# One bonus instruction for numerator and denominator, and a recomputed last maximum, in a linear attention of five engines

## The reference

```python
def step(carry, kv_t):
    p, q, o = carry
    kt, vt = kv_t
    no = jnp.maximum(o, u + kt)
    A = jnp.exp(o - no)
    Bc = jnp.exp(u + kt - no)
    y = (A * p + Bc * vt) / (A * q + Bc)
    no2 = jnp.maximum(w + o, kt)
    A2 = jnp.exp(w + o - no2)
    B2 = jnp.exp(kt - no2)
    return ((A2 * p + B2 * vt, A2 * q + B2, no2), y)
```

## Time and profile before

| | us |
|---|---|
| median of 3 runs | 6002.13 |
| lowest, highest | 5991.86, 6011.43 |
| profiled execution, its own time | 6008.11 |
| its span, first to last instruction | 6006.3 |
| attention stage in it | 1698 to 3718 |
| VectorE busy over the span | 4211.5 (70%) |
| TensorE busy over the span | 4937.5 (82%) |

### The profile page before, as it was taken

The page is one execution under the profiler, slowest core; times in us unless marked ns, Lnnn a source line. Parts: engine busy times, 40 slices in busy tenths (PEclk is TensorE's granted clock), DMA queues, the critical chain, the costliest instruction groups (busy, mean ns, idle before and its releaser), DMA issues. The chain is left out here.

```text
span 6006.3 us, 77285 instructions
## 1 busy us (share of the span) xinstructions
PE 4937.5 (82%) x23504; PEld 3954.3 (66%) x23504; DVE 4211.5 (70%) x5193; ACT 3702.6 (62%) x6950; POOL 3425.7 (57%) x2796
## 2 busy tenths in 40 slices
PE   5969999958866766767667673788899999999999
PEld 5969999847632443433334332676788888888888
DVE  4427777789849898888888885897555555555555
ACT  0016666545557888888888884565565665656565
POOL 0019999835549687777777872454444444444444
PEclk9979999979988988888889886999999999999999
DMA  6977777578840223213212122887422322322320
GB/s 170 264 187 197 193 196 205 148 185 255 245 104 11 68 52 76 65 43 88 54 44 65 44 65 56 233 268 226 105 69 54 82 60 56 86 56 54 88 54 24
DMA packets 389868, 689.60 MB, mean 115 GB/s; under 512 B 22399, under 2 KB 347986, under 8 KB 370194
## 3 DMA queue, kind: packets, MB, share of 16 engines
q1 hardware_dynamic: 335184, 529.89, 36.6%
q10 hardware_dynamic: 54386, 156.21, 7.3%
HBM read 452.17 MB, written 233.87 MB: 114 GB/s over the span
## 5 line engine op out<-in xcount | busy, mean ns | idle before, releaser
L1543 POOL TENSOR_TENSOR hidden_part<-hidden_whole,hidden_part 128x448 fp32r<-128x448 f32 x672 | 751.5, 1154 | 1025.9 <-ACT hidden_part L1508 1025.7
L661 POOL TENSOR_TENSOR omni_in_part<-omni_norm,omni_in_part 118x448 fp32r<-118x448 f32 x384 | 466.0, 1215 | 555.5 <-ACT omni_in_part L723 539.7
L1412 PE MATMUL f_out_ps<-hidden_part,ffn_wv_parts 128*128 128x448 f32 (+1 forms) x3360 | 720.8, 370 | 0.7 <-POOL hidden_part L1543 0.7
L418 POOL TENSOR_TENSOR dw_band_part<-dw_band,dw_band_part 112x862 fp32r<-112x862 f32 x192 | 438.7, 2285 | 470.6 <-ACT dw_band_part L529 470.5
L1412 PEld LDWEIGHTS f_out_ps<-hidden_part,ffn_wv_parts 128*128 128x128 f32 (+1 forms) x3360 | 578.1, 177 | 103.7 <-POOL hidden_part L1543 35.1
L87 PE MATMUL omni_ps<-omni_in_part,omni_band_part 118*118 118x432 f32 (+1 forms) x1152 | 435.7, 378 | 236.2 <-DVE omni_band_part L693 218.4
L1217 POOL TENSOR_TENSOR input_times_v<-input_factor,v_all 128x448 f32<-128x448 f32 x336 | 419.6, 1249 | 362.8 <-ACT input_factor L1110 343.3
L1586 DVE TENSOR_SCALAR hidden_whole<-f_hid_ps 128x448 f32<-128x448 f32 x672 | 417.6, 622 | 250.5 <-POOL hidden_part L1543 155.9
L1039 PE MATMUL proj_ps<-mixT_low,kvr_weights_low 128*128 128x448 f32 x672 | 354.0, 611 | 203.9 <-ACT k_all L1101 174.1
L87 PE MATMUL dw_ps<-dw_in_part,dw_band_part 112*118 112x432 f32 (+3 forms) x1344 | 473.7, 352 | 57.4 <-POOL dw_in_part L488 57.4
L1041 PE MATMUL proj_ps<-mixT_ends,kvr_weights_ends 128*128 128x448 f32 x1008 | 515.3, 595 | 0.0
(11 more groups left out here) (183 smaller groups left out, 13650.6 us busy)
## 6 DMA issues: line engine op xcount, KB each, us to landing
dw_band<-flat SPq DMA_DIRECT2D x48, 1508.5 KB
xin<-x SPq DMA_DIRECT2D x16, 2352.0 KB, 13.1
x_pointwise<-xp ACTq DMA_DIRECT2D x16, 2352.0 KB, 18.9
dw_in<-x_pointwise SPq DMA_DIRECT2D x24, 1568.0 KB
y_gelu<-dw_out ACTq DMA_DIRECT2D x48, 784.0 KB
omni_in<-y_gelu SPq DMA_DIRECT2D x48, 784.0 KB
att_mix<-omni_out ACTq DMA_DIRECT2D x48, 784.0 KB
residual_pairs<-y_gelu SPq DMA_DIRECT2D x16, 2352.0 KB, 11.9
```

The costliest lines, as they stand in the source:

```text
L418: eng.tensor_tensor(rounded(p[1]), wt[u][0:parts, cc, :], p[0], ALU.subtract).then_inc(band_split, 1)
L661: pool.tensor_tensor(rounded(p[1][:, :, :]), z[u][:, cc], p[0][:, :, :], ALU.subtract).then_inc(in_split, 1)
L1412: return pe.matmul(bank, rounded(w), rounded(x), start=start, stop=stop)
L1543: pool.tensor_tensor(rounded(kk[n % 2][1][:, h, :]), whole[h % KW][:, :], kk[n % 2][0][:, h, :], ALU.subtract).then_inc(kl_ready, 1)
```

## The change

1. **One bonus instruction.** `input_factor` and `input_times_v` become the two halves of one buffer `input_factors` of 128 x 2 x 448, four of them. A single `scalar_tensor_tensor` over both halves and both PSUM banks does what L1282 and L1285 did. It waits for both scans, and one semaphore, `added`, takes the place of `d_done` and `n_done`; the log waits for it, and the division needs only the inverse. `weigh` now waits for the division of four units before instead of two (column units still also for the last division of the tile's rows).
2. **Row units recompute the last maximum.** From the second row unit of a pass on, the scan covers 449 cells: it starts one pixel earlier, from the former unit's maximum before its last pixel, and so writes cell 0 itself. The copy is gone. Column units keep the copy, and their scan now starts from the cell just copied, behind a wait for it.
3. **Buffers.** `run_max` has 3 buffers instead of 4 and `decay_exponent` 1 instead of 2; GpSimd waits for the former unit's exponential before it writes it. GpSimd's wait for the carried cell remains only for the units that still have a memset or a copy (`carried`).

```diff
-        O = [m.sb(f"run_max{u}", [128, 1 + QT]) for u in range(RING)]
-        AX = [m.sb(f"decay_exponent{u}", [128, QT]) for u in range(2)]
+        ORING = 3
+        O = [m.sb(f"run_max{u}", [128, 1 + QT]) for u in range(ORING)]
+        AX = m.sb("decay_exponent", [128, QT])
         A = [m.ps(f"decay_factor{u}") for u in range(2)]
-        E = [m.sb(f"input_factor{u}", [128, QT]) for u in range(RING)]
-        EV = [m.sb(f"input_times_v{u}", [128, QT]) for u in range(2)]
+        EE = [m.sb(f"input_factors{u}", [128, 2, QT]) for u in range(RING)]
+        E, EV = [[t[:, n, :] for t in EE] for n in range(2)]
...
+        carried = [unit for unit in line if unit.q == 0 or not unit.rows]
+        def follows(unit):
+            return unit_of[unit.tile, unit.rows, unit.q - 1]
...
             def log(unit):
-                e = E[unit.slot][:, :]
-                act.wait_ge(d_done, unit.count())
+                e = E[unit.slot]
+                act.wait_ge(added, unit.count())
                 act.activation(e, e, ACT.Ln).then_inc(ln_done, 1)
...
-                pool.wait_ge(carry_done, unit.count())
-                need(pool, a_exp, unit.count(2))
-                pool.tensor_tensor(AX[unit.slot % 2][:, :], o[:, 0:QT], o[:, 1:1 + QT], ALU.subtract
-                                   ).then_inc(a_arg, 1)
+                if unit in carried:
+                    pool.wait_ge(carry_done, carried.index(unit) + 1)
+                need(pool, a_exp, unit.count(1))
+                pool.tensor_tensor(AX[:, :], o[:, 0:QT], o[:, 1:1 + QT], ALU.subtract).then_inc(a_arg, 1)
 
             def weigh(unit):
                 if unit.rows:
                     pool.wait_ge(bank_read, entry["project", unit.tile, unit.q, 1] + 1)
-                    need(pool, wkv_done, unit.count(2))
+                    need(pool, wkv_done, unit.count(RING))
...
             def divide(unit):
-                pool.wait_ge(n_done, unit.count())
                 pool.wait_ge(rec_done, unit.count())
...
-                o = O[unit.slot]
+                o = unit.run
                 if unit.q == 0:
                     dve.memset(o[:, 0:1], NEG).then_inc(carry_done, 1)
-                    start = NEG
+                    dve.tensor_tensor_scan(o[:, 1:1 + QT], free(unit.decay_ps, [[0, QT]]), k, NEG, ALU.add, ALU.max
+                                           ).then_inc(o_done, 1)
+                elif unit.rows:
+                    first = unit.q * QT - 1
+                    k = kS[:, unit.tile % 2, first:first + 1 + QT]
+                    dve.wait_ge(o_done, follows(unit).count())
+                    dve.tensor_tensor_scan(o[:, :], free(unit.decay_ps, [[0, 1 + QT]]), k,
+                                           follows(unit).run[:, QT - 1:QT], ALU.add, ALU.max).then_inc(o_done, 1)
                 else:
-                    former = unit_of[unit.tile, unit.rows, unit.q - 1]
-                    dve.wait_ge(o_done, former.count())
-                    start = O[former.slot][:, QT:QT + 1]
-                    dve.tensor_copy(o[:, 0:1], start).then_inc(carry_done, 1)
-                dve.tensor_tensor_scan(o[:, 1:1 + QT], free(unit.decay_ps, [[0, QT]]), k, start,
-                                       ALU.add, ALU.max).then_inc(o_done, 1)
+                    dve.wait_ge(o_done, follows(unit).count())
+                    dve.tensor_copy(o[:, 0:1], follows(unit).run[:, QT:1 + QT]).then_inc(carry_done, 1)
+                    dve.wait_ge(carry_done, carried.index(unit) + 1)
+                    dve.tensor_tensor_scan(o[:, 1:1 + QT], free(unit.decay_ps, [[0, QT]]), k, o[:, 0:1],
+                                           ALU.add, ALU.max).then_inc(o_done, 1)
...
             def sums(unit):
                 dve.wait_ge(e_exp, unit.count())
                 dve.wait_ge(a_exp, unit.count())
                 need(dve, kept, unit.count(1))
-                need(dve, d_done, unit.count(1))
-                scan(unit, 0, Q, E[unit.slot]).then_inc(q_done, 1)
+                need(dve, added, unit.count(1))
+                scan(unit, 0, E[unit.slot]).then_inc(q_done, 1)
                 dve.wait_ge(ev_done, unit.count())
-                need(dve, n_done, unit.count(1))
-                scan(unit, 1, P, EV[unit.slot % 2]).then_inc(p_done, 1)
+                scan(unit, 1, EV[unit.slot]).then_inc(p_done, 1)
 
             def outputs(unit):
-                e, ev = E[unit.slot][:, :], EV[unit.slot % 2][:, :]
+                both = EE[unit.slot][:, :, :]
                 dve.wait_ge(q_done, unit.count())
-                dve.scalar_tensor_tensor(e, e, unit.bonus, Q, ALU.mult, ALU.add
-                                         ).then_inc(d_done, 1)
                 dve.wait_ge(p_done, unit.count())
-                dve.scalar_tensor_tensor(ev, ev, unit.bonus, P, ALU.mult, ALU.add
-                                         ).then_inc(n_done, 1)
+                dve.scalar_tensor_tensor(both, both, unit.bonus, PQ[:, :, 0:QT], ALU.mult, ALU.add
+                                         ).then_inc(added, 1)
                 dve.tensor_copy(last[unit.slot][:, :], PQ[:, :, QT - 1]).then_inc(kept, 1)
```

More of the change, by code:

```diff
@@ L1109, in input_factor @@
                 act.wait_ge(e_arg, unit.count())
-                act.activation(E[unit.slot][:, :], E[unit.slot][:, :], ACT.Exp).then_inc(e_exp, 1)
+                act.activation(E[unit.slot], E[unit.slot], ACT.Exp).then_inc(e_exp, 1)
             def decay_factor(unit):
@@ L1114, in decay_factor @@
                 need(act, p_done, unit.count(2))
-                act.activation(A[unit.slot % 2][:, 0:QT], AX[unit.slot % 2][:, :], ACT.Exp, bias=unit.decay
-                               ).then_inc(a_exp, 1)
+                act.activation(A[unit.slot % 2][:, 0:QT], AX[:, :], ACT.Exp, bias=unit.decay).then_inc(a_exp, 1)
             def log(unit):
-                e = E[unit.slot][:, :]
-                act.wait_ge(d_done, unit.count())
+                e = E[unit.slot]
+                act.wait_ge(added, unit.count())
                 act.activation(e, e, ACT.Ln).then_inc(ln_done, 1)
             def invert(unit):
-                e = E[unit.slot][:, :]
+                e = E[unit.slot]
                 act.wait_ge(ln_done, unit.count())
@@ L1201, in exponents @@
                 pool.wait_ge(o_done, unit.count())
-                o, e = O[unit.slot], E[unit.slot]
-                k = kS[:, unit.tile % 2, unit.q * QT:(unit.q + 1) * QT] if unit.rows else e[:, :]
-                pool.tensor_tensor(e[:, :], k, o[:, 1:1 + QT], ALU.subtract).then_inc(e_arg, 1)
-                pool.wait_ge(carry_done, unit.count())
-                need(pool, a_exp, unit.count(2))
-                pool.tensor_tensor(AX[unit.slot % 2][:, :], o[:, 0:QT], o[:, 1:1 + QT], ALU.subtract
-                                   ).then_inc(a_arg, 1)
+                o, e = unit.run, E[unit.slot]
+                k = kS[:, unit.tile % 2, unit.q * QT:(unit.q + 1) * QT] if unit.rows else e
+                pool.tensor_tensor(e, k, o[:, 1:1 + QT], ALU.subtract).then_inc(e_arg, 1)
+                if unit in carried:
+                    pool.wait_ge(carry_done, carried.index(unit) + 1)
+                need(pool, a_exp, unit.count(1))
+                pool.tensor_tensor(AX[:, :], o[:, 0:QT], o[:, 1:1 + QT], ALU.subtract).then_inc(a_arg, 1)
             def weigh(unit):
@@ L1261, in run_max @@
-                dve.tensor_tensor_scan(o[:, 1:1 + QT], free(unit.decay_ps, [[0, QT]]), k, start,
-                                       ALU.add, ALU.max).then_inc(o_done, 1)
-            def scan(unit, n, state, added):
-                start = last[unit_of[unit.tile, unit.rows, unit.q - 1].slot][:, n:n + 1] if unit.q else 0.0
-                return dve.tensor_tensor_scan(state, A[unit.slot % 2][:, 0:QT], added[:, :], start,
+                    dve.tensor_tensor_scan(o[:, 1:1 + QT], free(unit.decay_ps, [[0, QT]]), k, NEG, ALU.add, ALU.max
[6 more added lines that the diff above has]
+                                           follows(unit).run[:, QT - 1:QT], ALU.add, ALU.max).then_inc(o_done, 1)
+                else:
+                    dve.wait_ge(o_done, follows(unit).count())
[3 more added lines that the diff above has]
+                                           ALU.add, ALU.max).then_inc(o_done, 1)
@@ L1267, in scan @@
+            def scan(unit, n, added_in):
+                start = last[follows(unit).slot][:, n:n + 1] if unit.q else 0.0
+                return dve.tensor_tensor_scan(PQ[:, n, 0:QT], A[unit.slot % 2][:, 0:QT], added_in, start,
                                               ALU.mult, ALU.add)
```

21 lines of the change are left out of this document (10 added, 11 removed).

## The result

The changed kernel takes 6030.41 us (median of 6 runs, 6015.88 to 6048.04) against 5997.91 us (median of 6, 5991.2 to 6011.43): a ratio of 1.0056, interval [1.0037, 1.0075]. It is slower by some 33 us, more than the 18 us that can be told from no change. The range of the prediction (5986 to 6040) holds it; its likeliest number, 6016, is 14 us too low. The prediction stood on a median of 6002.13 for the kernel before, which took 4 us less beside the changed one, so in the change itself it is off by more: +14 us said, +33 measured.

What follows compares the result with a forecast made beforehand. No engine bounds the whole span; VectorE is busiest in attention, with 0.53 of units exposed. Its +17 us became +9, plus +5 for the later log: +14 on 6002.13, so 6016 us, range 5986 to 6040.

Steps and rivals of the forecast that it cites:

- Scan to merged instruction is then 1.14 + 0.035 = 1.175: On VectorE, distance in us from numerator scan's start to merged instruction: scan's length plus a gap, against 1.04 before.
- In the new order none does: No further wait stands behind the last one before the merged instruction, so its gap was taken as 0.035, not 0.22 us.
- +8 us: Merged bonus instruction on VectorE: +0.025 us a unit over 336 units, before allowing for idle time.
- the sum +17: All VectorE changes if every unit were exposed: +8 merged instruction, -9 row copy, +18 column wait, in us.
- The rival of the dear wait: Waiting behind a PSUM write costs VectorE 0.22 us instead of 0.035, giving 6063 us; chance 0.08.
- Row copy -9 and column wait +17 or 18 us: Last maximum on VectorE: 144 row units lose a copy, -9 us; 144 column scans wait for theirs, forecast +18 us.
- The share of exposed time, 0.53: Estimated part of attention units paced by VectorE, 177 of 336, where extra VectorE work lengthens the stage.
- plain steps: Nine attention steps without image projection and residual; VectorE was said to pace 12 of 14 units in each.
- The residual steps: Fifteen attention steps that also project an image out and add its residual; VectorE was said to pace 4.5 of 14 units.
- The later log, +5 us: ScalarE's log at the sigmoid of nine steps starts 0.6 us later, waiting for the merged instruction: +5 us.
- everything is exposed: Idle time on VectorE moves with its work instead of swallowing it: +31 us, 6033 us; chance 0.25.
- The free wait: Rival: waiting behind the numerator scan costs VectorE nothing extra, so merging saves 0.11 us a unit, 5982 us; chance 0.12.

Runs made afterwards that it cites:

- e1: Changed kernel with row copies as before and each maximum scan started, without a wait, from the former unit's own cell; stage +24.4 us over before, ratio 1.0057.
- e3: Kernel before, with the first bonus instruction also waiting for the numerator's scan; stage +25.7 us over before, ratio 1.0047.
- e10: Kernel before, with three spare copies of the last sums added behind the bonus instructions of each unit; stage +28.3 us over before, ratio 1.0059.
- e4: Kernel before, with the log waiting for both bonus instructions and VectorE's work untouched; stage +12.2 us over before, ratio 1.0019.
- e2: Changed kernel with the two bonus instructions of before, keeping the new maximum and smaller buffers; stage +0.7 us over before, ratio 1.0013.

## Why the prediction was right, and where its sum was off

**The sign, and the step that gave it.** The merged instruction saves a fixed part of 0.10 us a unit and exposes the end of the scan that it now waits for. This is shown: e1 carries nearly all of the loss, and the distances are those of the argument.

**Its price was under a third of the real one.** "Scan to merged instruction is then 1.14 + 0.035 = 1.175" was 1.23. I took the 0.035 of the earlier trace rows, where an instruction has one wait, for one that has two. "In the new order none does" is true as it stands, since the wait for the denominator's scan is ahead of the one that comes last and not behind it; what failed is the conclusion that it is therefore free. It costs 0.06 us even when it is long satisfied. So +8 us became +30, and the sum +17 became +38. The rival of the dear wait had the right suspicion and the wrong cause (PSUM) and size.

**The maximum.** Row copy -9 and column wait +17 or 18 us: both distances as predicted; together they came to +1 us in the stage.

**The share of exposed time, 0.53, was too high.** The doses give 0.35 (e3) and 0.40 (e10), and both still hold steps that the clock made longer. I was right that plain steps are paced by VectorE: 12 of 14 units (0.86) said, 0.84 measured by e10. The residual steps, which I gave 4.5 of 14 units, pass on next to nothing of VectorE's time; what they did gain is the clock's. My sum had 17 x 0.53 = 9 us; the real one is a larger raw cost at a smaller share, some 1.3 us (1.6 x 0.84) in each of nine plain steps, 12 us.

**The later log, +5 us, was right for the place that I priced.** The stall at the sigmoid is 0.65 us in nine plain steps, 6 us.

**What the sum left out is TensorE's clock.** The granted clock stands nowhere in it, although it was in the rows. The longer plain steps went with a stretch at half clock in each of the seven residual steps of the second kind, 8.4 us by the pair in e4. 12 + 6 + 8 = 26 is near the 25.6 of the stage, each term an estimate from a like kernel. It is tempting to add e4's 12 us to 0.35 x 38 = 13, but both hold part of the clock's loss, so that this too gives 25 is chance.

**Luck.** That the range held owes something to luck. Raw cost was too small by 21 us and the clock's 8 us were missing, against a share that was too large. The measured change is over twice the forecast one.

**The rival "everything is exposed"** named 6033 us and is nearest in number, but not in mechanism: under half of VectorE's time is exposed. Its raw sum of 17 us was too small and its share of 1 too large. The free wait fell: the distance is 1.23 and not 1.04. The Trainium skill's rule that a semaphore between costs nothing extra (VectorE: DVE Perf Modes, "The DRAIN you can't avoid") is contradicted here twice, by 0.13 us for the first wait and 0.06 for the second. What was costed at nothing held, by e2's +0.7 us, for the smaller buffers.

**Open.** The whole time grew by 33 [22, 45] us and the stage by 25.6; whether the other 7 are scatter of the other stages can't be said. Nor is it shown what makes the granted clock fall in the residual steps of one kernel and not of another.

## What to carry to other kernels

Before merging two instructions, ask what stands directly ahead of each: the first of a pair may run while the input of the second is still on its way, and the merged one can't. Price a wait from a row with the same number of waits, and drop those that another implies. Price the lateness of what a merged instruction releases apart from its length: at the sigmoid it cost half as much as the time did. And before giving VectorE the blame for a longer step, compare the granted clock of the steps: two steps of one kernel, with the same work, differ here by 1.2 us.

## What was unexpected of the hardware

- A satisfied second wait on the same VectorE instruction costs 0.06 us if the instruction has to wait at all (gap 0.10 with two waits, 0.04 with one).
- A result in PSUM is no later for a waiting reader than one in SBUF: 0.04 us behind either, for 448 elements.
- A stretch of 3.3 us at a granted clock of 0.50 instead of 1.00 on TensorE makes a residual step of 87 us longer by 1.2 us, in two steps of one kernel in which VectorE's timeline is the same to 0.02 us up to there (e4). In the changed kernel, with its longer plain steps, all seven second residual steps have it.
- Fewer and longer instructions left VectorE's busy time in the stage as it was (1697 to 1695 us) while the stage grew by 26 us.
